# Causal attention with a mixture of experts: two heads in one output product of 128 rows, heads divided by their denominators beforehand

## The reference

```python
xn = layernorm(x)                          # x: 4 batches x 1024 tokens x 128
q, k, v = heads(rms(xn) * gamma @ w_qkv)   # 16 heads of 64 columns
attn = softmax(causal(q @ k.T * 64**-0.5)) @ v
out = attn_of_all_heads @ w_out            # 1024 columns (16 x 64) to 128
return x + out + layernorm2(xn + top2_of_8_experts(xn))
```

## Time and profile before

| | us |
|---|---|
| timed median of 3 runs (lowest, highest) | 1583.55 (1583.36, 1583.85) |
| the profiled execution: time, span | 1578.72, 1577.0 |
| PE busy, share of the span | 1453.9, 92% |
| DVE, ACT, POOL busy | 1076.1, 1067.4, 904.9 |
| granted TensorE clock, mean of the span | 0.968 of full speed |

### The profile page before, as it was taken

One profiled execution on the slowest core, in us unless ns is written; L12 is line 12 of the kernel. 1 busy time (PEld: TensorE's weight loads), 2 busy tenths in 40 slices (PEclk: granted clock), 3 DMA queues, 4 the chain that ended last, 5 costly groups with the idle time before them and its releaser, 6 DMA issues.

```text
span 1577.0 us, 33357 instructions
## 1 busy us (share of the span) xinstructions
PE 1453.9 (92%) x9130; PEld 1128.0 (72%) x9131; DVE 1076.1 (68%) x2341; ACT 1067.4 (68%) x2590; POOL 904.9 (57%) x923
## 2 busy tenths in 40 slices
PE   3569999599999999999999999999999999999998
PEld 3458888477777777777777777777777777777776
DVE  6655555458866876687658776876687668766883
ACT  2536656277776777777767777777777777777775
POOL 0761000167665766676657666766676667666766
PEclk9669999699999999999999999999999999999999
DMA  8122111111111111111111111111111111111111
GB/s 308 48 83 72 52 58 48 40 38 38 33 28 41 38 33 28 41 38 33 28 39 40 33 28 39 40 33 28 39 40 33 28 40 39 33 28 41 37 28 54
DMA packets 58807, 72.86 MB, mean 46 GB/s; under 512 B 7400, under 2 KB 44560, under 8 KB 58640
## 3 DMA queue, kind: packets, MB, share of 16 engines
q1 hardware_dynamic: 40720, 52.57, 14.0%
q10 hardware_dynamic: 13824, 9.86, 2.0%
q0 software_dynamic: 4096, 8.40, 1.8%
HBM read 20.47 MB, written 16.52 MB: 23 GB/s over the span
## 4 chain that ended last, share of the span: by engine, by line
PE 67%; DVE 6%; issue 4%; ACT 3%; DMA 1%; SPq 0%; DVEq 0%; POOLq 0%; POOL 0%; ACTq 0%
PE max_ps L1291 9%; PE score_ps L1316 8%; PE score_ps L1317 8%; PE misc_ps L1350 8%; PE head_ps L1333 7%; PE head_ps L1337 7%; PE head_ps L1335 7%; PE misc_ps L1267 3%; PE max_ps L1294 2%; PE score_ps L1319 2%; DVE q_a L1125 2%; PE misc_ps L1261 2%; ACT p_hi L1082 1%; PE misc_ps L1300 1%; PE misc_ps L1263 1%
## 5 line engine op out<-in xcount | busy, mean ns | idle before, releaser
L1033 POOL TENSOR_TENSOR p_lo<-probs,p_hi 128x512 fp32r<-128x512 f32 (+3 forms) x768 | 773.7, 1022 | 432.0 <-ACT p_hi L1082 426.2
L1082 ACT ACTIVATE probs<-score_ps 128x512 f32<-128x512 f32 (+3 forms) x768 | 375.3, 489 | 250.8 <-PE score_ps L1319 170.9
L1135 DVE TENSOR_REDUCE row_max<-max_ps 128x1 f32<-128x128 f32 (+7 forms) x512 | 386.8, 756 | 171.6 <-PE max_ps L1294 161.0
L1082 ACT ACTIVATE p_hi<-score_ps 128x512 fp32r<-128x512 f32 (+3 forms) x768 | 373.1, 486 | 0.0
L1333 PE MATMUL head_ps<-p_hi,v_hi 128*65 128x512 f32 (+3 forms) x768 | 295.6, 385 | 0.3 <-POOL p_lo L1033 0.3
L1316 PE MATMUL score_ps<-q_a,k_a 128*128 128x512 f32 (+3 forms) x768 | 267.8, 349 | 14.0 <-issue 10.9
L1317 PE MATMUL score_ps<-q_b,k_b 65*128 65x512 f32 (+3 forms) x768 | 267.3, 348 | 0.0
L1291 PE MATMUL max_ps<-k_a,q_a 128*128 128x384 f32 (+5 forms) x768 | 250.1, 380 | 16.4 <-DVE row_max L1135 12.6
L1337 PE MATMUL head_ps<-p_lo,v_hi 128*65 128x512 f32 (+3 forms) x768 | 259.4, 338 | 0.0
L1335 PE MATMUL head_ps<-p_hi,v_lo 128*64 128x512 f32 (+3 forms) x768 | 259.0, 337 | 0.0
L1316 PEld LDWEIGHTS score_ps<-q_a,k_a 128*128 128x128 f32 x768 | 145.4, 189 | 60.0 <-issue 17.4
(11 more groups left out here) (170 smaller groups left out, 2105.6 us busy)
## 6 DMA issues: line engine op xcount, KB each, us to landing
k_a<-k_a SPq DMA_DIRECT2D x64, 256.0 KB, 3.8
q_b<-q_a SPq DMA_DIRECT2D x64, 256.0 KB, 4.3
sorted_x<-zeros SPq DMA_DIRECT2D x13, 384.0 KB, 16.1
w_raw<-sorted_x SPq DMA_DIRECT2D x26, 192.0 KB, 2.5
sorted_y<-result ACTq DMA_DIRECT2D x78, 64.0 KB, 1.6
acc<-in_L_attn_x_dram SPq DMA_DIRECT2D x4, 512.0 KB, 6.9
w_raw<-in_L_ffn_W_dram ACTq DMA_DIRECT2D x1, 2048.0 KB, 23.1
q_b<-shift SPq DMA_DIRECT2D x128, 2.0 KB
```

The lines of the kernel that those rows point to most:

```text
L1033: pool.tensor_tensor(p_lo[:, slot, 0:w], probs[:, slot, 0:w], p_hi[:, slot, 0:w].bitcast(F32), ALU.subtract).then_inc(p_split, 1)
L1082: ins = act.activation(p[:, (g * CH + c) % RING, 0:width], score_ps[(g * CH + c) % 2][:, 0:width], ACT.Exp, scale=SCALE)
L1135: dve.tensor_reduce(row_max[:, g % 2, t:t + 1], src, axes, ALU.max).then_inc(max_taken, 1)
```

## The change

The two heads of a batch are joined. Before, every g had its own output product with 65 rows; after, a batch has one product over 128 rows (64 of each head), in two units of four tiles of 128x128 instead of twice three units. That needs heads that are divided already. So ACT copies `head_ps` to `raw`, and the denominators go through a chain that stands at fixed distances (in chunks) behind the last chunk of a half: fold (+5; a DMA spreads row 64 of `raw` to 16 rows of 32), invert (+7; a reciprocal on DVE), store (+8; a DMA to DRAM), spread (+10; a DMA that copies the 512 inverses to 64 rows, 128 KB), normalise (+12; one DVE product of 64x512 into `heads`). The three DMAs are issued by ACT. There are 128 halves.

The y unit of the first 512 tokens stands at c=6 of the even g behind its batch, that of the second at c=1 of the odd g that follows. The shift of c=1 then comes right behind it. The loop's boundary moves from c=11 of g=0 to c=2 of g=1 (`CUT` 11 to 14), and the ring of `probs` shrinks from 6 to 4 slots.

```diff
-            probs = sb(ph2, "probs", [P, RING, BANK])
+            PROBS = 4
+            probs = sb(ph2, "probs", [P, PROBS, BANK])
-            heads = sb(ph2, "heads", [HEAD + 1, 2, SEQ])
+            raw = sb(ph2, "raw", [HEAD + 1, 2, BANK])
+            heads = sb(ph2, "heads", [P, 2, SEQ])
-            wo = sb(ph2, "wo", [HEAD + 1, 2, D + 1])
+            wo = sb(ph2, "wo", [P, D])
+            CHAIN = [("fold", 5), ("invert", 7), ("store", 8), ("spread", 10), ("normalise", 12)]
-            Y_AT = [6, 9, 10]
-            y_units = [(0, 3), (3, 3), (6, 2)]
-            CUT = 11
+            Y_AT = {(0, 6): 0, (1, 1): 1}
+            CUT = 14
...
+                for kind, lag in CHAIN:
+                    if at >= lag and (at - lag) // CH < final and (at - lag) % CH in LAST:
+                        order.append((kind, (at - lag) // CH, LAST.index((at - lag) % CH)))
...
+                        act.dma_start(den[:, half], raw[HEAD:HEAD + 1, half].rearrange("o (f n) -> o f n", f=FOLD)
+                                     ).then_inc(den_folded[half], 16)
...
+                        act.dma_start(inv_rows[half].rearrange("(f n) -> f n", f=FOLD), inv[:, half]
+                                     ).then_inc(inv_stored[half], 16)
...
+                        act.wait_ge(inv_stored[half], hp * (16 * G) + (16 * g + 16))
+                        act.dma_start(scale[:, half], inv_rows[half].partition_broadcast(HEAD)
+                                     ).then_inc(scale_spread[half], 16)
...
+                                if order is not before_loop or g * CH + c >= PROBS:
+                                    act.wait_ge(p_split, n_chunk(hp, g, c) - PROBS + 1)
...
-                        dve.reciprocal(rden[:, u % 2, 0:tiles], src[:, :, D]).then_inc(recip_done, 1)
...
-                            ins = dve.scalar_tensor_tensor(out=row, in0=src[:, t, 0:D], scalar=rden[:, u % 2, t:t + 1],
-                                                           in1=row, op0=ALU.mult, op1=ALU.add)
+                        dve.wait_ge(scale_spread[half], hp * (16 * G) + (16 * g + 16))
+                        dve.tensor_tensor(heads[s * HEAD:(s + 1) * HEAD, i, cols], raw[0:HEAD, half], scale[:, half],
+                                          ALU.mult).then_inc(normalised, 1)
...
+                        dve.tensor_tensor(acc[:, toks], misc_ps[u % 2][:].rearrange("p (t d) -> p t d", t=GROUP),
+                                          acc[:, toks], ALU.add).then_inc(y_added, 1)
...
+                        pe.wait_ge(normalised, n_half(hp, 2 * p + 1, n) + 3)
...
+                            ins = pe.matmul(dst[:, t * D:(t + 1) * D], heads[:, p % 2, q0:q0 + P], wo[:],
+                                            start=True, stop=True)
```

More of the change, by code:

```diff
@@ L756, in attention_and_experts @@
         pv_done = sem("pv_done")
-        heads_out = [sem(f"heads_out{i}") for i in range(2)]
-        recip_done = sem("recip_done")
+        raw_out = sem("raw_out")
+        den_folded = [sem(f"den_folded{i}") for i in range(2)]
+        inverted = sem("inverted")
+        inv_stored = [sem(f"inv_stored{i}") for i in range(2)]
+        scale_spread = [sem(f"scale_spread{i}") for i in range(2)]
+        normalised = sem("normalised")
         y_added = sem("y_added")
@@ L903, in plan @@
                 order = []
-                for at in range(CUT, G * CH + (LAG if last else CUT)):
+                for at in range(CUT, G * CH + CUT):
                     order += beside(at // CH, at % CH, last)
                 if last:
-                    order += [(kind, G - 1, n) for n in range(len(y_units)) for kind in ("y", "add")]
+                    order += [(kind, BATCH - 1, n) for n in range(2) for kind in ("y", "add")]
                 return numbered(order, MISC0)
@@ L997, in _ @@
                 def _(pool):
-                    pool.memset(wo[:], 0.0).then_inc(mask_zeroed, 1)
                     for i in range(2):
@@ L1091, in walk @@
                                 shifts(hp, g, c, u)
+                            elif kind == "fold":
+                                fold_denominator(hp, g, c)
+                            elif kind == "store":
+                                store_inverse(hp, g, c)
+                            elif kind == "spread":
+                                spread_inverse(hp, g, c)
                             elif kind == "pv" and c in LAST:
@@ L1095, in walk @@
                                 act.wait_ge(pv_done, n_chunk(hp, g, c) + 1 + RING)
-                                act.activation(heads[:, g % 2, cols], head_ps[0:HEAD + 1, cols],
-                                               ACT.Copy).then_inc(heads_out[half], 1)
+                                act.wait_ge(normalised, n_half(hp, g, half) + 1)
+                                act.activation(raw[:, half], head_ps[0:HEAD + 1, cols],
+                                               ACT.Copy).then_inc(raw_out, 1)
                     run(walk, act)
@@ L1249, in misc_bank @@
                             kind, g, n = misc_units(plan(False))[u - MISC0 - 2]
-                            misc_read(hp, kind, g - (BATCH if kind == "project" else G), n)
+                            misc_read(hp, kind, g - (G if kind == "shift" else BATCH), n)
                         return misc_ps[u % 2]
@@ L1326, in values @@
                         pe.wait_ge(p_split, n_chunk(hp, g, c) + 1)
-                        if j == 0:
-                            pe.wait_ge(heads_out[half], hp * G + (g + 1))
+                        if j == 0 and (started or g):
+                            pe.wait_ge(raw_out, n_half(hp, g, half) - 1)
                         if c == 0:
```

95 lines of the change are left out of this document (46 added, 49 removed).

## The result

The changed kernel took **1677.2 us** (median of 4 runs, 1671.9 to 1686.2) against 1583.7 before: 1.059 times, with a 95% interval of 1.054 to 1.064. It is 93 us slower, where I had forecast 11 us faster, and it lies outside the range. The profiled execution has a span of 1679.0 us and a granted clock of 0.951 (before 0.968).

A forecast was written before the change was run, and what follows sets the result against it. PE's order was taken as the clock, other engines close behind. Terms -53.6 + 19.5 + 7 + 2 + 5 + 4 + 5 = -11 us, applied to the median of 1583.55, gave 1572.5 us; range 1555 to 1601.

The forecast's parts named there:

- What bounds the kernel: Even stretch from 316 to 1570 us: PE's order is the clock, busy 1217 of 1254 us, idling 37.
- PE's products, -53.6: Output products between chunks: 1,008 old records (107.5 us) give way to 62 new units (53.9 us), saving 53.6 us.
- The shift behind v, +19.5: At c=1 of odd g, PE's shift waits for v's low part: 30 times 0.65 us, +19.5 us.
- The copies, +7: PE reaches the next odd g 0.84 us earlier and waits there for copies, eight times: +7 us.
- ACT's three DMAs, taken at 0: Three DMA issues a half fit ACT's 338 us of idling, and the store lands after 1.6 us: 0.
- The smaller ring of probs, taken at 0: Exponentials wait for the low part four chunks back, which PE's next product with v awaits anyway: 0.
- POOL and the boundary, +4: POOL and the loop boundary moved to c=2, where DVE has less slack: together +4 us, bounds 0 and 13.
- Normalise, +2 and +5: DVE's normalise, 0.68 us, exceeds free time at c=3: +2 us in 31 even g's, +5 us in eight g=3's.
- Rival A: Spread lands late; at c=3 of even g DVE stands before the scale, PE behind: +28 us, 1600, chance 0.20.
- Rival B: Normalise takes 1.56 us instead of 0.68 because POOL's subtraction is running: +27 us, 1600 us, chance 0.18.
- The slow row: Profile row of a DVE operation with two SBUF inputs, 1.56 us where one alike in shape took 0.68.
- The tail, +5: From ACT's last copy to DVE's last addition: 8.6 us instead of 3.9, +5 us, bound above +12.

The follow-up runs named there:

- e5: Changed kernel without the division by the denominators, the y unit of c=1 at c=4 behind the shift, the loop's boundary at c=5: 1568.0 us.
- e1: Changed kernel with the y unit of c=1 put ahead of the projection of v: 1674.6 us.
- e6: Changed kernel, division kept, with the y unit of c=1 at c=4 behind the shift and the loop's boundary at c=5: 1624.9 us.
- e8: Changed kernel with the loop's boundary alone moved from c=2 to c=5 of g=1: 1662.8 us.
- e2: Changed kernel with the spread alone issued by SyncE instead of ACT: 1658.2 us.
- e3: Changed kernel without the division (no fold, invert, store, spread or normalise), places of y and boundary kept: 1617.4 us.
- e4: Kernel before with the loop's boundary alone moved from c=11 of g=0 to c=2 of g=1: 1583.6 us.
- e9: Changed kernel with y at c=6 and c=4, boundary at c=5, spread issued by SyncE, store, spread and normalise at distances 8, 11, 14: 1638.3 us.
- e13: As e9, with the first y at c=8 instead of c=6: 1604.9 us.
- the spread combine: Kernel before with the second layer norm's 21 pieces on DVE spread over g=3 to g=7 instead of g=3 to g=5: 1563.5 us.

## Why the prediction was wrong

- **What bounds the kernel: right for before, wrong for what came.** PE's order was the clock, with 37 us of idling. But that slack was so thin on three sides (ACT, DVE, the boundary) that any wait put into another engine's order came through. I priced PE well and the covers badly.
- **PE's products, -53.6: the term is right, its yield is not.** There are 512 records, and 31 of the units take 0.87 us from their start to the next start, as I had taken; but PE's busy time in the even stretch did not fall at all (above), against what I had named as the test of this term. Without the chain and with y behind the shift (e5) it fell by 39. What ate it is what the waits bring with them: the lower clock, some 27 us, and the stops, some 26, both estimates. I had put a wait at its own length, and nothing for either.
- **The shift behind v, +19.5: right in size.** 30 waits, 24.5 us. But trading this wait for another, of 12.2 us, at the same place (e1) returned nothing, while moving y out of c=1 altogether, with the boundary (e5, e6), returned about 50 us, of which the boundary alone is some 14 (e8). I had priced a wait by its length; what hung on its place, the boundary and the half clock behind, was larger.
- **The copies, +7: not seen.** PE's waits from 316 us on have no line for a copy, in either kernel.
- **ACT's three DMAs, taken at 0: the step that failed first.** I compared ACT's idle time in all (338 us) with the issues, and took the store's landing from a row of 1.6 us. Away from the copies it was mostly less, 1.35; beside the copies of the even g it was 3.4 in the median. An engine that works in order has no use for its idle time in all: it stood behind one store with exponentials queued, and PE stood behind those, 36 us, where I had none; taking most of that away (e2) gave 19 us of time back. With the rest of the chain, of which I had only priced normalise and the tail, it is 60 us (e3).
- **The smaller ring of probs, taken at 0: open.** In the changed kernel ACT's exponentials wait 13.5 us, in 13 waits, for POOL's low part, where before they never did. Without the chain (e3), on the same ring, it is 1.4 us. No run changes the ring alone.
- **POOL and the boundary, +4: too small.** The boundary went from 1.8 to 3.2 us, six times shown, with a stretch of half clock at each. e4 shows that c=2 isn't at fault by itself.
- **Normalise, +2 and +5: wrong in kind.** At c=3 of an even g nothing was waited for: all of them took 0.68 to 0.69 us there but one at 0.93, and none of the 31 between chunks waited for the scale. DVE's waits were elsewhere, at c=11, in front of the scale, and they hardly show in PE's; where normalise itself held PE up is shown only with the transfers given time (e9, e13). Rival A had the mechanism (the scale late, DVE in front of it) at the wrong place and for the wrong reason, the spread, which came in time, instead of the store ahead of it.
- **Rival B, in part.** Normalise's mean is 974 ns instead of 680:

```profile
L1228 DVE TENSOR_TENSOR heads<-raw,scale 64x512 f32<-64x512 f32 x128 | 124.7, 974 | 84.3 <-DMA scale<-inv_rows 83.1
```

  By start and end times in the trace, with the two over 2 us left out, 85 normalisations began while POOL's subtraction ran and took 1.06 us on average; 41 did not and took 0.68, all within 0.67 to 0.69. One of the first kind, with the subtraction beside it:

```profile
783.69 2.71 POOL L1041 TENSOR_TENSOR p_lo<-probs,p_hi 128x512 fp32r<-128x512 f32 x2 [0.37 <-ACT p_hi L1108]
```

```profile
785.19 1.75 DVE L1228 TENSOR_TENSOR heads<-raw,scale 64x512 f32<-64x512 f32 x1
```

  The second of POOL's two ends at 786.40, normalise 0.54 us later. Of the 85, 78 ended 0.54 to 0.56 us after a subtraction's end, however long before it they had begun. This is what the Trainium skill, "SBUF — State Buffer", section "SBUF: two separate sides", says of two SBUF inputs beside a GpSimd operation that reads SBUF: the later one stands still until the other is done. Here the trace agrees, but for the 0.54 us, which is less than the 0.68 that normalise takes alone. The slow row that I had left open fits too: in the trace of before, one of that group begins at 749.77, beside a subtraction that ends at 750.78, and ends at 751.32, 0.54 us later. It cost normalise 0.3 us a time in the mean, not 0.88. But the same meeting made the low part of the weights late, 1.8 us of PE at the start of g=6 in all but one of seven pairs, which no rival had.
- **The tail, +5: right.** From the end of the last copy to raw (1665.60) to the last addition (1675.36) are 9.8 us, estimated 8.6, before 3.9.

So the step that failed is the one that took ACT's three DMAs at 0 (they held PE up for 36 us, and moving one of them won 19), and with it the rule that a wait costs PE its own length and no more (the 53.6 us of the products didn't come back). What stays open: how much of the 93 us each of these is alone, since the experiments show that the waits cover one another (e1 gives 0 and e2 19, while e5 and e6 give about 50 and dropping the division 57 to 60); and why the boundary is long where it is.

## What to carry to other kernels

Where one engine's order is the clock, price a new step not by its share of an engine's idle time but by who stands behind it in that engine's order, at each place. A chain of small transfers is as long as its landings in the worst neighbourhood, here beside 1 MB of copies, and a wait removed pays only if the next one, a chunk on, isn't waiting for the same engine. Each stop can cost more than its length, as here the lower clock and the stops ate the 53.6 us that the products gave back. Look for such next bounds in the kernel before: the 20 us of the spread combine were to be had without the change.

## What the runs showed of the hardware

The store of 2 KB to DRAM landed after 1.3 to 5.6 us: after 3.1 or more, 3.4 in the median, in the 30 cases in which the copies had been issued on another queue within 6 us before, and after 1.34 to 1.38 in 25 of 34 without them. The 128 KB read back landed within 2.8 to 3.4. The small transfer was the uncertain one. A VectorE operation with two inputs in SBUF that met a subtraction on GpSimd ended 0.54 to 0.56 us after it in 78 of 85 cases. And moving the loop's boundary from c=11 to c=2 cost 0 in the kernel before, while moving it from c=2 to c=5 gave back some 14 us in the changed one.
